# A graph layer with experts on one core: edge keys read back by broadcast instead of transposed, and another order of the opening

## What is computed

```
xn = layernorm(x)
mask = full((384, 384), -inf); mask[src, dst] = softplus(etw)[type - 1]   # the last edge of a pair wins
mask[i, i] = softplus(etw)[3] where the diagonal was not set
gnn: q, k, v = xn @ w.T + b;  q2, k2, v2 = (q, k, v) @ wi.T + bi
     softmax(q2 k2 / 8 + mask) v2, 16 heads;  @ wo.T + bo
mix: q, k, v = xn @ w.T, elu + 1 on q and k, linear attention, @ wo.T + bo
x = x + gnn + mix
x = x + experts(layernorm(x))      # 32 experts of 512, the best 4 of each row, sigmoid gates
```

## Time and profile before

| | us |
|---|---|
| median of 3 runs | 980.32 (980.06 to 980.93) |
| profiled execution, its own time | 980.56 |
| its span, first to last instruction | 978.5 |
| PE busy | 893.7 (91%) |
| DVE busy | 662.4 (68%) |
| ACT busy | 528.5 (54%) |
| POOL busy | 319.3 (33%) |
| mean granted clock of TensorE | 0.961 |

### The profile page before, as it was taken

The page is one execution under the profiler, slowest core; times in us unless marked ns, Lnnn a source line. Parts: engine busy times, 40 slices in busy tenths (PEclk is TensorE's granted clock), DMA queues, the critical chain, the costliest instruction groups (busy, mean ns, idle before and its releaser), DMA issues.

```text
span 978.5 us, 13956 instructions
## 1 busy us (share of the span) xinstructions
PE 893.7 (91%) x4482; PEld 750.1 (77%) x4482; DVE 662.4 (68%) x1050; ACT 528.5 (54%) x685; POOL 319.3 (33%) x292
## 2 busy tenths in 40 slices
PE   3889999999999999898984899998999999999993
PEld 3788889989989999544774788787888887777772
DVE  6676766653434534576486699888799987778880
ACT  3343322232323322475412688888788887777870
POOL 0603445544430000598001133432233332322331
PEclk9899999999999999999975899999999999999997
DMA  8424332233334333100391599999999999999931
GB/s 303 161 89 133 129 130 87 87 125 120 114 120 175 129 129 129 44 1 1 137 379 57 209 350 358 370 346 354 331 349 361 354 360 321 341 333 320 331 111 21
DMA packets 40453, 203.00 MB, mean 207 GB/s; under 512 B 12880, under 2 KB 13136, under 8 KB 18400
## 3 DMA queue, kind: packets, MB, share of 16 engines
q1 hardware_dynamic: 26496, 186.66, 51.5%
q0 software_dynamic: 13200, 15.03, 6.3%
q10 hardware_dynamic: 720, 0.83, 0.2%
HBM read 203.33 MB, written 21.15 MB: 229 GB/s over the span
## 4 chain that ended last, share of the span: by engine, by line
PE 52%; DMA 26%; POOL 7%; DVE 7%; issue 3%; ACT 2%; POOLq 0%; ACTq 0%; DVEq 0%; SPq 0%
PE ps L1099 15%; PE ps L1100 15%; PE ps L1101 15%; DMA raw_x<-in_keys 12%; POOL pr L387 6%; DMA out_dram<-etmp,pcol 4%; DMA xg<-xt_dram,gcol 3%; DMA out_dram<-ysb,pcol 3%; DMA raw_x<-in_values 2%; PE ps L1282 1%; PE ps L1129 1%; PE ps L1213 1%; DVE wl L832 1%; DMA c_all<-in_c_all 1%; ACT wh L640 1%
## 5 line engine op out<-in xcount | busy, mean ns | idle before, releaser
L630 ACT ACTIVATE wh<-raw 128x1024 fp32r<-128x1024 f32 x88 | 93.1, 1060 | 254.3 <-PE ps L1101 243.5
L784 DVE TENSOR_TENSOR wl<-raw,wh 128x1024 fp32r<-128x1024 f32 x88 | 110.0, 1253 | 158.8 <-ACT wh L630 158.6
L545 POOL DMA_INDIRECT plane<-code,idx x96 | 100.0, 1042 | 119.8 <-DMA plane<-code,idx 81.9
L1099 PE MATMUL ps<-wh_x,hTh 128*128 128x512 f32 x248 | 102.9, 415 | 0.0
L1099 PE MATMUL ps<-wh,xgTh 128*128 128x512 f32 x248 | 98.2, 396 | 0.0
L1101 PE MATMUL ps<-wh,xgTl 128*128 128x512 f32 x248 | 97.9, 395 | 0.0
L1100 PE MATMUL ps<-wl,xgTh 128*128 128x512 f32 x248 | 97.9, 395 | 0.0
L1101 PE MATMUL ps<-wh_x,hTl 128*128 128x512 f32 x248 | 97.8, 394 | 0.0
L1100 PE MATMUL ps<-wl_x,hTh 128*128 128x512 f32 x248 | 97.4, 393 | 0.0
L387 POOL TENSOR_SCALAR pr<-pr,mx 128x384 f32<-128x384 f32 x48 | 58.7, 1240 | 104.0 <-DVE mx L356 104.0
L1099 PE MATMUL ps<-xnh,wh 128*128 128x384 f32 x256 | 88.0, 344 | 2.1 <-issue 2.1
(11 more groups left out here) (220 smaller groups left out, 2022.4 us busy)
## 6 DMA issues: line engine op xcount, KB each, us to landing
raw<-in_keys SPq DMA_DIRECT2D x34, 1024.0 KB, 14.1
raw_x<-in_values SPq DMA_DIRECT2D x34, 1024.0 KB, 15.8
raw_x<-in_keys SPq DMA_DIRECT2D x30, 1024.0 KB, 14.7
raw<-in_values SPq DMA_DIRECT2D x30, 1024.0 KB, 14.0
raw<-in_w_v SPq DMA_DIRECT2D x8, 1024.0 KB, 4.8
raw<-in_w_q SPq DMA_DIRECT2D x8, 1024.0 KB, 4.9
raw<-in_w_k SPq DMA_DIRECT2D x8, 1024.0 KB, 4.8
raw<-in_w_mq SPq DMA_DIRECT2D x4, 1024.0 KB, 7.9
```

What stands on the lines that cost most here:

```text
L545: nc.gpsimd.indirect_dma_start(plane[m], bass.IndirectOffsetOnAxis(idx[:, g:g + 1].bitcast(U32), 0), code[:, g:g + 1], None, bounds_check= ...
L630: nc.scalar.activation(wh[:, s % SUB], raw[:, c % RAW, 2 * (s % 2):2 * (s % 2) + 2, :], ACT.Copy)\
L784: nc.vector.tensor_tensor(wl[:, s % SUB], raw[:, (s // 2) % RAW, 2 * (s % 2):2 * (s % 2) + 2, :], wh[:, s % SUB].bitcast(F32), ALU.subtrac ...
L1099: nc.tensor.matmul(o, ah, bh_, start=start, stop=False)
```

## The change

What it does:

- The dup jobs leave the order and PE's work. The 96 keys columns are transposed at once (one 128 x 96 transpose before the xT transposes), copied by ACT to `key_t`, stored by POOL to an HBM tensor `key_dram`, and read back by POOL, 2048 keys at a time, into every partition (`key_rows`, three buffers of 8 KB a partition in A1, `rows_of_keys`). DVE compares against these rows (`same_keys`), four columns after each weight split from sub 8 on, eight after sub 12.
- ACT waits for all six index groups before it writes v0's first bank.
- SP starts the weights right behind x. ACT's queue brings the identity and the edges first, the rest of the constants after x. PE waits for the identity before the transposes and for the rest before mq0.
- xT0 and xT1 become one run of 24 transposes, tile by tile, into eight banks.
- DVE makes the key between the first and second tile of x, and the first split right after xn; ACT's and DVE's splits are placed anew in xT1 and mq0.
- Both planes are filled by POOL at the start with six stores. The diagonal is written by three indirect DMAs from the type weight; the diagonal tile on DVE is gone. The edge values move from mq1 to mk0.
- POOL adds `bo` to `mbo` and then the sum to `acc` (four adds in place of six), after the first index group.

The core of the diff:

```diff
-    names = ["xT0", "xT1", "mq0", "dup0", "mq1", "dup1", "mk0", "dup2", "mk1", "dup3", "mv0", "dup4",
-             "mv1", "dup5", "lin", "v0", "mix0", "mix1", "mix2", "v1", "mT0", "mT1", "mo0", "mo1",
+    names = ["xT0", "xT1", "mq0", "mq1", "mk0", "mk1", "mv0", "mv1", "lin", "v0", "mix0", "mix1", "mix2", "v1", "mT0", "mT1", "mo0", "mo1",
...
         def _(sp):
             for t in range(NT):
                 sp.dma_start(acc[:, t, :], x[t * P:(t + 1) * P, :]).then_inc(s_x[t], 16)
-            sp.wait_ge(s_const, 16 * N_CONST)
...
         def _(pool):
+            nc.gpsimd.memset(none[:, :], NEG).then_inc(s_none, 1)
+            pool.wait_ge(s_none, 1)
+            for m in range(2):
+                for t in range(NT):
+                    pool.dma_start(plane_rows[m][:, t, :], none[:, :]).then_inc(s_init, 16)
+            def rows_of_keys(k):
+
+                g = GROUP * GROUPS[k]
+                pool.dma_start(key_rows[k % 3][:, :], key_dram[g * P:(g + GROUP) * P, :].rearrange("e o -> o e").to_broadcast([P, GROUP * P]))\
+                    .then_inc(s_rowk[k % 3], 16)
+
+            pool.wait_ge(s_keyc, 1)
+            pool.dma_start(key_dram.rearrange("(g p) o -> g (p o)", p=P), key_t[0:EC, :]).then_inc(s_keyd, 16)
+            pool.wait_ge(s_keyd, 16)
+            for k in range(3):
+                rows_of_keys(k)
+            pool.wait_ge(s_idx, 1)
+            rows_of_keys(3)
             pool.wait_ge(s_rows, 16 * N_ROWS)
             pool.wait_ge(s_xn, NT)
-            for t in range(NT):
-                nc.gpsimd.tensor_tensor(acc[:, t, :], acc[:, t, :], bo_b[:, :], ALU.add).then_inc(s_pch, 1)
-                pool.wait_ge(s_pch, t + 1)
+            nc.gpsimd.tensor_tensor(mbo_b[:, :], mbo_b[:, :], bo_b[:, :], ALU.add).then_inc(s_pch, 1)
+            pool.wait_ge(s_pch, 1)
             for t in range(NT):
                 nc.gpsimd.tensor_tensor(acc[:, t, :], acc[:, t, :], mbo_b[:, :], ALU.add).then_inc(s_bias, 1)
-            pool.wait_ge(s_base, NT)
-            pool.dma_start(plane_rows[0], mask[:, :, :]).then_inc(s_init, 16)
+            pool.wait_ge(s_init, 16 * 2 * NT)
+            pool.wait_ge(s_weight, 1)
             for t in range(NT):
-                pool.dma_start(plane_rows[1][:, t, :], none[:, :]).then_inc(s_init, 16)
-            pool.wait_ge(s_init, 16 * (NT + 1))
+                nc.gpsimd.indirect_dma_start(plane[0], bass.IndirectOffsetOnAxis(diag[:, t:t + 1].bitcast(U32), 0), w4[:, 4, 3:4], None,
+                                             bounds_check=N * N - 1, oob_is_err=False).then_inc(s_init, 16)
+            pool.wait_ge(s_init, 16 * 3 * NT)
+            pool.wait_ge(s_idx, 2)
+            rows_of_keys(4)
             for k in range(0, len(GROUPS), 2):
                 pool.wait_ge(s_idx, k + 2)
                 for q in range(GROUP):
+                    if k == 0 and q == GROUP // 2:
+                        pool.wait_ge(s_idx, 3)
+                        rows_of_keys(5)
...
         def _(act):
-            act.dma_start(ei[:, :, :], edges).then_inc(s_const, 16)
+            act.dma_start(call[:, 0:P], C["all"][:, 0:P]).then_inc(s_ident, 16)
+            act.dma_start(ei[:, :, :], edges).then_inc(s_edges, 16)
             act.dma_start(w4[:, 0, :], etw.to_broadcast([P, 4])).then_inc(s_const, 16)
+            act.wait_ge(s_x[NT - 1], 16)
+            act.dma_start(call[:, P:], C["all"][:, P:]).then_inc(s_const, 16)
             act.dma_start(col[:, :, :], cols).then_inc(s_const, 16)
             act.dma_start(sel[:, :, :], selT).then_inc(s_const, 16)
-            act.dma_start(call[:, :], C["all"]).then_inc(s_const, 16)
...
+            act.wait_ge(s_keyt, 1)
+            nc.scalar.activation(key_t[0:EC, :], ps[0][0:EC, 0:P], ACT.Copy).then_inc(s_keyc, 1)
             split(2)
...
+                        if name == "v0" and b == 0:
+                            act.wait_ge(s_idx, len(GROUPS))
...
+            def same_keys(u):
+
+                k, c = u // 4, u % 4
+                if c == 0:
+                    dve.wait_ge(s_rowk[k % 3], 16 * (k // 3 + 1))
+                for q in range(4 * c, 4 * c + 4):
+                    g = GROUP * GROUPS[k] + q
+                    link(nc.vector.scalar_tensor_tensor(junk[:, :], key_rows[k % 3][:, q * P:(q + 1) * P], ef[:, 3, g:g + 1],
+                                                        after[:, :], ALU.is_equal, ALU.mult, accum_out=dup[:, g:g + 1]))
+                if c == 3:
+                    gs = slice(GROUP * GROUPS[k], GROUP * GROUPS[k] + GROUP)
+                    nc.vector.scalar_tensor_tensor(idx[:, gs], dup[:, gs], FAR_EDGE, ef[:, 3, gs], ALU.mult, ALU.add).then_inc(s_idx, 1)
 
             def split(upto):
...
+                    if s >= jobs["mq1"]["sub_end"]:
+                        for u in range(units[0], min(units[0] + (2 if s == jobs["mk0"]["sub_end"] else 1), 4 * len(GROUPS))):
+                            same_keys(u)
+                            units[0] += 1
...
-                if name == "mq1":
+                if name == "mk0":
                     dve.wait_ge(s_ra, 1)
-                    link(nc.vector.scalar_tensor_tensor(w4[:, 4, :], w4[:, 0, :], 0.0, w4[:, 3, :], ALU.max, ALU.add))
+                    link(nc.vector.tensor_scalar(diag[:, :], cst["own"][:, 0:NT], float(N + 1), None, ALU.mult))
+                    nc.vector.scalar_tensor_tensor(w4[:, 4, :], w4[:, 0, :], 0.0, w4[:, 3, :], ALU.max, ALU.add).then_inc(s_weight, 1)
+                    dve.wait_ge(s_weight, 1)
                     edge_values(link)
-                    empty_planes(link)
+                if not name.startswith("xT"):
+                    split(j["sub_end"] + LEAD)
...
+                if name == "xT0":
+
+                    pe.wait_ge(s_key, 1)
+                    nc.tensor.transpose(ps[0][0:EC, 0:P], ef[:, 3, :], ident).then_inc(s_keyt, 1)
+                    pe.wait_ge(s_keyc, 1)
+                    for t in range(NT):
+                        pe.wait_ge(s_xn, t + 1)
+                        for o in range(DC):
+                            last = nc.tensor.transpose(ps[o][:, t * P:(t + 1) * P], xn[:, t, o * P:(o + 1) * P], ident)
+                            if t == NT - 1:
+                                last.then_inc(s_bank, 1)
+                    pe.wait_ge(s_const, 16 * N_CONST)
+                    continue
```

More of the change, by code:

```diff
@@ L249, in gps_layer_kernel @@
         s_key = sem("s_key")
+        s_edges = sem("s_edges")
+        s_keyt = sem("s_keyt")
+        s_keyc = sem("s_keyc")
+        s_keyd = sem("s_keyd")
+        s_rowk = [sem(f"s_rowk{r}") for r in range(3)]
         s_s = sem("s_s")
@@ L655, in _ @@
                     continue
-                if name == "dup0":
+                if name == "mq1":
                     act.wait_ge(s_spl, 1)
@@ L672, in _ @@
                         split(j["sub_end"] + LEAD + 1)
+                    if name == "xT1" and b in (0, 2):
+                        split(3 + b // 2)
                     base = j["base"]
@@ L822, in _ @@
                     row_stats(t, k)
+                if t == 0:
+                    dve.wait_ge(s_edges, 16)
+                    link(nc.vector.tensor_copy(ef[:, 0:3, :], ei[:, :, :]))
+                    nc.vector.scalar_tensor_tensor(ef[:, 3, :], ef[:, 0, :], float(N), ef[:, 1, :], ALU.mult, ALU.add).then_inc(s_key, 1)
             norms(0, NT, xn, s_xn, 1)
+            split(1)
             colno = {n: k for k, n in enumerate(COLS)}
@@ L840, in _ @@
                     continue
-                if not name.startswith("xT"):
-                    split(j["sub_end"] + LEAD)
                 half = int(name[-1]) if name[-1].isdigit() else 0
@@ L868, in _ @@
                         bank_filled(dve, j, b)
-                    if name.startswith("dup"):
-                        for q in range(4):
-                            g = GROUP * GROUPS[half] + 4 * b + q
-                            last = nc.vector.scalar_tensor_tensor(junk[:, :], pb[:, q * P:(q + 1) * P], ef[:, 3, g:g + 1],
-                                                                  after[:, :], ALU.is_equal, ALU.mult, accum_out=dup[:, g:g + 1])
-                            if q < 3:
-                                link(last)
-                        last.then_inc(s_free, 1)
-                        dve.wait_ge(s_free, j["first"] + b + 1)
-                        if b == 3:
-                            gs = slice(GROUP * GROUPS[half], GROUP * GROUPS[half] + GROUP)
-                            nc.vector.scalar_tensor_tensor(idx[:, gs], dup[:, gs], FAR_EDGE, ef[:, 3, gs], ALU.mult, ALU.add).then_inc(s_idx, 1)
-                    elif base in ("xT", "mT"):
+                    if base in ("xT", "mT"):
                         hi, lo = (xnh, xnl) if base == "xT" else (mbh, mbl)
@@ L1123, in _ @@
                 bk = [ps[4 * j["set"] + b] for b in range(4)]
[L1124 to L1133 removed]
+                if base == "mT":
+                    pe.wait_ge(s_free, end["mix2"])
```

(1 more changed line is left out.)

63 lines of the change are left out of this document (25 added, 38 removed).

## The result

The changed kernel takes **963.9 us** (median of 4 runs, 960.9 to 965.4), the kernel before beside it 980.2 (4 runs, 977.6 to 980.9). The ratio is 0.983, 95% interval 0.981 to 0.985: 16.3 us less. Forecast were 961.5, with 953 to 973 as range. The profiled execution took 964.72, 15.8 less than the one of before (980.56); its span is 961.8, 16.7 less.

A forecast was written before the change was run, and what follows sets the result against it. TensorE, busy 91% of the span, was taken as the bound, with opening gains carried to the end. Terms of -24.3, -1.9, +2.2, +1.4, +2.3 and +1.2 sum to -19.1 from 980.56: 961.5 us, range 953 to 973.

The forecast's parts named there:

- transposes and their waits out: From mq0 to lin: one undisturbed job's 16.8 us times five plus mq0's 18.7, 102.7 against 127.0, 24.3 us less.
- opening: Before mq0: weights and first split come earlier, x arrives as now, 1.9 us less.
- pause on wl: In mk1: bias adds on GpSimd hold VectorE's edge values and so sub 12's split, 2.3 us more.
- half clock behind it: After the pause for sub 12's split: half a chance of the slow PE clock, 1.2 us more.
- lin waits for mv's copies: Before lin: PE waits for mv1's three copies, which dup5 transposes hid, 2.2 us more.
- v0 and the mixes: At v0 and mix1: ScalarE's first v0 write waits for the last index group, 1.4 us more.
- a rival (22%): Opening: late constants queued behind other loads; PE starts 2.5 us later, 964, or 10 later, 972; chance 22%.
- VectorE's term: From 61 to 71 us: GpSimd's bias adds lock VectorE out, delaying sub 12's split by 2.3 us.
- VectorE keeps PE fed: Rival, mk0 to lin: adds fall between splits, no clock lost, compares nearer 0.26; 957, or 956; chance 13%.
- VectorE is the bound: Rival, mk0 to mv1: compares cost 0.55 each, three or four us lost twice, slow clock after each, 970; chance 8%.
- The scatter: GpSimd: first scatter from about 84.5 us, planes back at about 304, 11 us of slack, no cost.
- The slower rival: Scatter becomes the end: each us late costs one, slower than before from a start at 115; at 120, 985; chance 6%.

The follow-up runs named there:

- e7: Kernel before without its six dup jobs, indices from constants: mq0 to lin 103.55 us instead of 127.0, attention 23.3 us earlier, whole time 18.7 less.
- e3: Changed kernel with the four bias adds ahead of the wait for the first index group: attention 3.0 us earlier.
- e10: Changed kernel with the three key row loads held until the constants have landed: mq0 at 23.68 against 23.74 us, attention 3.0 us earlier.
- e1: Changed kernel with PE's wait for the late constants moved from before mq0 to before mk0: attention 4.8 us earlier.
- e2: Changed kernel with the six plane stores issued behind the three key row loads: attention 5.2 us earlier.
- e11: Changed kernel with ScalarE issuing the rest of the constants at once, not after x has landed: 960.2 us.
- e8: Kernel before with SP no longer waiting for the constants ahead of its weight loads: ratio 1.000 [0.999, 1.001].
- e9: Changed kernel with the first scatter waiting for the fifth index group: attention 11.9 us later, time 0.2% under the kernel before [0.996, 1.000].
- e12: Changed kernel itself, run once more: 965.9 us (963.0 to 967.3).
- e5: Changed kernel with the compares begun behind sub 4 instead of sub 8, scatters waiting for the edge values, sixth row load earlier: attention 6.1 us earlier.
- e4: Changed kernel without its 96 compares, indices from two constants: attention 7.1 us earlier, whole time not comparable.

## Why the prediction was right, and where it was not

Up to attention, term by term (us, profiled executions):

```
                                             forecast   measured
transposes and their waits out                 -24.3      -24.3   e7: 103.55 - 0.87 = 102.7
mq0's slow start twice as long                  -         +1.3   mq0 to mk0: 36.59, e7 35.32
opening                                         -1.9       +2.2   23.74 - 21.57
pause on wl                                     +2.3       +1.7   its 1.3 and 0.4 around it, e3
half clock behind it                            +1.2        0
lin waits for mv's copies                       +2.2       +1.9
half clock behind that                           -         +1.7   e10 has none
v0 and the mixes                                +1.4       +1.4
sum                                            -19.1      -14.1   400.97 - 386.85
expert stage and around it                       0        -1.7   964.72 - 980.56 + 14.1
```

**Right:** the mechanism. PE loses 96 transposes, two waits and the half clock behind each, and that is carried to the end. The first term came out to a tenth. It rests on one undisturbed job's length read from the earlier trace rows and multiplied by six, not on the sum of what goes. lin at 131.3 is outside the 122 to 128 that I gave, but inside the 132 from which the whole was to be called wrong.

**The step that failed: the opening.** I wrote 1.9 us less, and it was 2.2 more. Of these 4.1, the part about the shorter way from x to mq0 was nearly right: 1.4 faster, as e1 shows (5.57 against 6.98). Then x was 1.4 later; I had priced the plane stores at 1.3 "at worst" and chosen zero, hoping that the stores would yield. e2 shows that they don't. And PE waited 2.2 longer than e1 does for the constants, which I had as a rival (22%) at 2.5. So this rival was the truth in the opening, with its smaller price. That its 964 is also the measured time is luck: the opening was 4.1 off and not 2.5, and other terms made up for it. It was set against c_all's 7.9 us of the earlier trace rows. That was right for c_all (8.4), but c_all isn't the last: sel, 128 KB behind it on the same queue, took 12.4. The rule of the Trainium skill ("DMA: Bandwidth & Descriptors", "Queues, rings and completion order"), queues in turn by packets, gave me an estimate of about 17 for all of them. sel landed at about 23.7, and in e11 17.9 us from its issue: the measurement decides against that use of it. The rival's 22, served in the order of issue, was nearer, but e11 speaks against that order too: there sel was issued at 3.56, amid the weights, and landed at about 21.5. e8 shows that weights beside them delay the small loads, e2 that the plane stores do, and e10 takes the key rows out of the question. The bias rows (1.5 MB, on SP's queue) and the size of sel's pieces were not tested, and how the turns are really shared between the queues, no run here settles.

**The clock, priced at the wrong pauses.** I gave the pause on wl half a chance of a slow stretch, and the one before lin none. In the 14 traces the granted clock went to 0.50 at each of the ten pauses of 1.85 to 4.4 us ahead of mq0, and in seven of eight behind the 1.9 us one before lin where it exists (after, e1, e2, e3, e9, e11 and e12, not e10). From mq0 to attention it never did so at one of 1.4 or less. Length alone isn't a rule: behind the idle time before the transposes of xn, 6.6 to 7.1 us with the new opening and 14.6 to 15.9 with the old one, it was 1.00 in every trace. A slow stretch cost 1.4 or 2.7 us in mq0 and 1.7 at lin. This is what makes e1 and e2 worth more than their waits.

**VectorE's term** had the right cause, and 1.7 came where 2.3 was said. The adds ran 66.08 to 75.74 (58 to 75 was said), and four operations went through beside them, three of 2.3 us and one of 1.2. The page "SBUF — State Buffer", section "SBUF: two separate sides", of the Trainium skill has an exclusive lock there; 2.31, 2.33 and 2.38 us against 0.27, each as long as one add (7.16 / 3), agree with it, and e3 takes the adds away and finds 0.27. The prediction drew from the same rule that compares become targets; e5 bears it out, with 2.4 to 2.5 us beside an add. Elsewhere a compare took 0.35, the row of the same operation; "VectorE keeps PE fed" is out, for the waits for VectorE are 3.2 us in all up to lin, and so is "VectorE is the bound", by e3 against e4. That these were places in VectorE's order and not its load, e5 shows.

**The scatter** started at 88.7, not 84.5: GpSimd had the diagonal out by 80, then waited 8.1 us for the second index group, whose compares stand behind the edge values that the adds held (8.5 us earlier in e3), and a row load stands ahead of the first scatter. It is then in slack, as said. The slower rival's price was too high in e9: the 96 scatters took 203 us from first to last and not 215. Why is open: the kernel before, without any row loads, takes 210. And VectorE's 18.8 us of waiting cost PE 10.2, since splits and banks in hand covered 8.6. With one us for each us, the point where it turns slower than before lies near 131 (2.4 us more than 128.8; an estimate).

The last 1.7 us are the sum of 2.6 less from attention to the end of the span and 0.8 more outside it (2.9 against 2.1). The expert stage differs by as much between executions of one program, so no cause is claimed for them. They hid a part of the miss, and so did the median, 0.8 under the profiled execution: 5.0 us up to attention became 2.4. That is luck.

## What to carry to other kernels

When a block of work leaves the bounding engine, measure what stays by one undisturbed unit, and then ask of each neighbour what it was hiding: the two waits that came up here were copies and an index that the transposes had covered. A small load beside full queues can land 10 us and more after its issue (sel 12.4, against 7.2 before the change), so a wait on "all constants" belongs at the first use of the last one. Price a PE pause of about 2 us at its length and the half clock behind it; moving VectorE's filler work from the last possible place to an earlier one was worth 4.9 us, where deleting it was worth 6.0.

## What was not expected of the hardware

- A pause of 1.9 us before lin was followed by half clock seven times of eight, and each cost 1.7 us, nearly as much as the pause. Idle times of 6.6 us and more before the transposes were not.
- Loads of 20 KB (col, 10.6 us) and 128 KB (sel, 12.4) behind 451 KB (8.4) on one queue, beside four weight chunks of 1 MB at 16.4 us each; issued 8 us earlier they took 15.8 and 17.9.
- Stores of 192 KB, six at the start in place of three later, went from 3.1 to 9.9 us and cost x 1.4 us on another queue.
- Compares with both inputs in SBUF take 352 ns on average, the 350 of PSUM within 2 ns; beside a GpSimd add they take 2.4 us (e5).
